# One-hot gathers on TensorE: 12 of 26 columns with the penalty in three spare rows, in place of 10 or 11 columns with a ninth matmul

## The chip, the cores and the metric

The kernel runs on one NeuronCore of a Trainium2 chip. The metric is device time in microseconds (us) of one execution. The kernel before took 16193.71 us, the median of three runs (16133.8 to 16216.83).

## The reference

A graph of 12500 nodes with 16 features and 412500 edges, sorted by destination. Three edge-conditioned convolutions (NNConv) and one maximum aggregation, with residuals:

```
def _nnconv(x, src, dst, edge_attr, ew, eb, rw, rb):
    W = (edge_attr @ ew + eb).reshape(edge_attr.shape[0], x.shape[1], rw.shape[1])
    msg = jnp.einsum('ei,eio->eo', x[src], W)
    return segment_sum(msg, dst, num_segments=x.shape[0]) + x @ rw + rb

h = relu(layernorm(x))
for i in range(2): h = relu(batchnorm(nnconv_i(h)))
h = relu(nnconv_2(h));  x = x + h @ pred_w + pred_b
h = relu(layernorm(x))
x = x + segment_max(h[src] * weight, dst) @ W.T + b
```

`ew` has 8 edge features, so an edge's message is a sum over 8 features and a bias of a row of 9 x 16 values that depends on the source node alone.

## The kernel before, in words

The padded edges are 128 streams (one a partition) of 3224 edges. A chunk is 26 columns, 26 edges of each stream; there are 124 chunks, handled two at a time (slots 0 and 1). Every column needs for each of its 128 edges the row of the edge's source node. It gets it in one of two ways.

- The first columns (16 of 26 in the convolutions, 15 in the maximum) are gathered by GpSimd: one indirect DMA a column (line 541), from a table of 144 values a node in HBM (`conv_table`) or of 16 values a node (`max_table`). VectorE releases a slot's next gathers by writing `idx` (line 968), after it has read the gathered columns.
- The last columns (10 in the convolutions, `TP_CONV`; 11 in the maximum, `TP_MAX`) are picked on TensorE from `h`, which lies in SBUF as 128 lanes by 98 blocks of 128 nodes, split in two fp32r parts (`parts`). The 98 blocks are four zones of 25. For each column, `pe_step` multiplies a one-hot matrix over (lane, zone) with the 25 blocks of that zone, for four zones and two parts: eight matmuls of 400 columns (line 712). The sum holds, for each edge, its lane's row in 25 blocks. A ninth matmul in bf16 (line 714) puts a very large negative number on the 24 wrong blocks, and VectorE takes the maximum over the blocks (`pick`, line 845). In PSUM four banks take turns, so step j waits for the pick of step j - 4.

In the convolutions a picked column has only `h`. `pe_turn` (line 723) transposes a half of the picked columns (a lot of five), ScalarE copies the transpose to `xeT` (`act_turn`, line 783), and `pe_product` (line 733) multiplies it with the edge weights, in pieces of three and two columns, fp32 in two passes each. VectorE multiplies these with the edge features (`lot_product`).

ScalarE makes the one-hot matrices for the next chunk of the same slot: four times an `Abs` of key minus lane number (line 592, the lane number a per-partition operand) and a `Relu` of 1 minus that (line 597, constants), 1408 wide whatever `TP_CONV` is, and the `Abs` for the ninth matmul (line 608). In order, `act_body` does: the first lot's `xeT` copy, the factors and flags, the store of the run, a wait until all steps of this chunk have left `hot_key` free, the one-hots of zones 0 and 1 (`hots_begin`), the second lot's `xeT` copy, and zones 2 and 3 (`hots_end`). TensorE in the same stretch does the first four steps of the next chunk, with the second lot's transpose after two of them, and then that lot's product.

The keys are rows of HBM (`key_rows`), broadcast by one DMA for two chunks to 128 partitions (`load_keys`, line 582), issued by SyncE once `hot_key` of both slots is written.

VectorE multiplies and sums the features and scans the chunk (line 952). After the 124 chunks `nodes` gathers each node's end of segment: 98 more gathers, in groups of 7 blocks (`GB`), and `node_product` makes the next table, again in groups of 7. All of the order is written out by hand.

## Time and profile before

| | before |
|---|---|
| median of 3 runs | 16193.71 us |
| span of the profiled execution | 10810.0 us |
| TensorE busy, share | 90% |
| GpSimd busy, share | 73% |
| ScalarE, VectorE busy, share | 65%, 61% |
| mean granted TensorE clock | 0.969 |

The span runs from the first to the last instruction of the one execution that was profiled. That execution's own time outside the span is in no view: only the span of 10810.0 us is. The runs' median is 5383.7 us above the span. Busy GpSimd time is that of the gathers' issue; about 0.3 us lie between two of them and count as idle. The trace has three stretches of 124 chunks for the convolutions, about 2510 us each, one of about 2380 us for the maximum, and about 200 us between two of them.

### The profile page before, as it was taken

The numbers are of one execution on the slowest core, as the hardware profiler recorded it, in microseconds if no ns is written. First come the engines' busy times: TensorE is split into PE (matmuls) and PEld (weight loads), VectorE is DVE, ScalarE is ACT, GpSimd is POOL, SyncE is SP. The second block draws the span as 40 slices with busy tenths as digits, with TensorE's granted clock in tenths as the row PEclk, the third lists the DMA queues.
The fourth block names the chain that finished last, engine by engine and source line by source line (L and its number), as shares of the span: only waits on it lengthen the run. The fifth ranks groups of instructions, "written<-read, shape, count | busy, mean of one in ns | idle before, by whom it ended". The sixth has DMA issues, their size and how long they took to land.

```text
span 10810.0 us, 169480 instructions
## 1 busy us (share of the span) xinstructions
PE 9676.4 (90%) x50106; PEld 8184.1 (76%) x50106; DVE 6568.9 (61%) x10058; ACT 7050.4 (65%) x7269; POOL 7931.6 (73%) x8306
## 2 busy tenths in 40 slices
PE   6999999998599999999849999999984999999994
PEld 4888888887488888888738888888873888888883
DVE  6677677776477677677646777776772444444442
ACT  3776776775367766767537767767763777777772
POOL 7777777777577777777757777777776777777776
PEclk9999999999799999999979999999997999999997
DMA  4333333333233333333323333333331222222221
GB/s 118 111 105 112 111 105 111 112 105 101 75 110 107 111 108 110 111 107 110 96 78 107 111 110 107 111 110 107 111 97 35 56 56 56 56 56 56 56 56 26
DMA packets 427085, 997.76 MB, mean 92 GB/s; under 512 B 167103, under 2 KB 266760, under 8 KB 395047
## 3 DMA queue, kind: packets, MB, share of 16 engines
q0 software_dynamic: 265664, 460.92, 18.3%
q1 hardware_dynamic: 161383, 536.39, 14.6%
q8 instruction: 16, 0.26, 0.0%
q14 instruction: 22, 0.18, 0.0%
HBM read 867.11 MB, written 129.62 MB: 92 GB/s over the span
## 4 chain that ended last, share of the span: by engine, by line
POOL 52%; issue 27%; DVE 10%; DMA 8%; PE 2%; DVEq 1%; POOLq 0%; ACT 0%; SPq 0%; ACTq 0%
POOL gathered L541 51%; DVE msg L927 8%; DMA gathered<-conv_table,idx 7%; PE pY L712 1%; DVE xe L845 1%; DVE idx L968 1%; PE pY L458 1%; DVEq L234 1%; POOL gathered L1108 1%; DVE gathered L270 0%; DMA conv_w<-in_conv_w 0%; DMA gathered<-scanned,idx 0%; DVE tmp L270 0%; PE pY L733 0%; PE pT L447 0%
## 5 line engine op out<-in xcount | busy, mean ns | idle before, releaser
L712 PE MATMUL pY<-part,hot_key 128*128 128x400 f32 x40672 | 8622.4, 362 | 438.0 <-DVE xe L845 409.4
L712 PEld LDWEIGHTS pY<-part,hot_key 128*128 128x128 f32 x40672 | 7322.9, 189 | 712.9 <-DVE xe L845 544.9
L541 POOL DMA_INDIRECT gathered<-conv_table,idx x5952 | 5639.3, 947 | 2030.4 <-issue 1810.9
L845 DVE TENSOR_REDUCE xe<-pY 128x16 f32<-128x400 f32 x5084 | 2834.9, 567 | 1348.9 <-PE pY L714 1334.0
L592 ACT ACTIVATE apart<-key_pair,zone_lane 128x1408 f16<-128x1408 f16 x1984 | 2804.2, 1461 | 670.5 <-PE pY L714 661.7
L597 ACT ACTIVATE hot_key<-apart 128x1408 fp32r<-128x1408 f16 x1984 | 2611.7, 1364 | 0.0
L541 POOL DMA_INDIRECT gathered<-max_table,idx x1860 | 1813.8, 975 | 611.5 <-issue 566.6
L270 DVE TENSOR_TENSOR gathered<-gathered,pT 128x2048 f32<-128x2048 f32 x372 | 851.2, 2288 | 1508.8 <-DMA gathered<-conv_table,idx 1508.8
L714 PE MATMUL pY<-near_mask,not_near 128*128 128x400 bf16 x5084 | 1747.0, 344 | 0.0
L927 DVE TENSOR_REDUCE msg<-gathered 128x256 f32<-128x2304 f32 x744 | 1559.4, 2096 | 0.2
L714 PEld LDWEIGHTS pY<-near_mask,not_near 128*128 128x128 bf16 x5084 | 488.6, 96 | 898.0 <-issue 898.0
L813 ACT COPY run_pair<-rows 128x416 f32<-128x416 f32 x496 | 491.8, 992 | 1019.3 <-DVE rows L952 1006.3
L783 ACT COPY xeT<-pT 80x128 f32<-80x128 f32 x744 | 186.6, 251 | 1363.1 <-PE pT L723 1359.2
L733 PE MATMUL pY<-edge_w,xeT 80*128 80x432 f32 (+1 forms) x2976 | 1024.5, 466 | 1.5 <-ACT xeT L783 1.5
L733 PEld LDWEIGHTS pY<-edge_w,xeT 80*128 80x128 f32 x2976 | 556.9, 193 | 261.2 <-issue 259.1
L608 ACT ACTIVATE not_near<-key_pair,zone_lane 128x1408 bf16<-128x1408 f16 x496 | 721.7, 1455 | 0.0
L270 DVE TENSOR_TENSOR gathered<-pY,pe_attr 128x432 f32<-128x432 f32 x1488 | 716.7, 524 | 3.6 <-ACT pe_attr L796 2.0
L270 DVE TENSOR_TENSOR msg<-gathered,pT 128x240 f32<-128x240 f32 x124 | 75.5, 609 | 715.0 <-DMA gathered<-max_table,idx 715.0
L952 DVE TENSOR_TENSOR_SCAN rows<-flags,msg 128x416 f32<-128x416 bf16 x496 | 503.5, 1015 | 0.1
L541 POOL DMA_INDIRECT gathered<-scanned,idx x392 | 373.6, 953 | 173.7 <-issue 116.7
L562 ACT COPY idx<-ends_i 128x7 int32 x56 | 10.6, 196 | 434.9 <-DVE agg L270 325.0
L447 PE MATMUL pT<-ident,hs 128*113 128x128 f32 x70 | 26.2, 388 | 287.2 <-ACT hs L422 284.1
(132 smaller groups left out, 1728.4 us busy)
## 6 DMA issues: line engine op xcount, KB each, us to landing
key_pair<-key_rows SPq DMA_DIRECT2D x248, 1408.0 KB, 6.3
scanned<-run_pair SPq DMA_DIRECT2D x248, 416.0 KB, 2.5
gathered<-conv_table,idx POOLq DMA_INDIRECT x5952
attr_pair<-in_attr SPq DMA_DIRECT2D x186, 208.0 KB
gathered<-max_table,idx POOLq DMA_INDIRECT x1860
conv_table<-gathered SPq DMA_DIRECT2D x24, 504.0 KB, 3.6
conv_table<-rows SPq DMA_DIRECT2D x18, 504.0 KB, 3.2
gathered<-scanned,idx POOLq DMA_INDIRECT x392, 2.3
```

What stands on the lines that cost most here:

```text
L270: return e.tensor_tensor(out, a, b, op)
L541: e.indirect_dma_start(out=G[s][:, t, 0:width], out_offset=None, in_=table[:, :], in_offset=bass.IndirectOffsetOnAxis(ap=idx[s][:, t:t + 1 ...
L592: e.activation(apart[k][:, :], keys[s][:, :], ACT.Abs, bias=zone_lane[:, z:z + 1]).then_inc(s_abs.sem, 1)
L597: e.activation(hot_key[s][:, z, :], apart[k][:, :], ACT.Relu, bias=1.0, scale=-1.0).then_inc(s_abs.sem, 1)
L608: e.activation(not_near[s][:, :], nears[s][:, :], ACT.Abs, bias=zone_lane[:, ZONES:ZONES + 1], scale=FAR).then_inc(s_hotk[s].sem, 1)
L712: e.matmul(pG[bank], hot_key[s][:, z, at:at + P], part[:, z * NEAR:(z + 1) * NEAR, :], start=(z == 0 and k == 0), stop=False)
L714: e.matmul(pG[bank], not_near[s][:, at:at + P], near_mask[:, :, :], start=False, stop=True).then_inc(s_gath.sem, 1)
L733: ins = e.matmul(pE[:, q, 0:m * ROW], xeT[:, :], edge_w[:, k * ROW:(k + m) * ROW], start=True, stop=True)
L813: e.copy(run[s][:, :, :], scan[s][:, :, :].rearrange("p d t -> p t d")).then_inc(s_run[s].sem, 1)
L845: e.tensor_reduce(xe[s][:, j * D:(j + 1) * D], pG[j % BANKS].rearrange("p (r d) -> p d r", d=D), AX.X, ALU.max).then_inc(s_pick.sem, 1)
L927: return mark(e.tensor_reduce(rows_of(a, b), g[:, a:b, :].rearrange("p t (d f) -> p t d f", f=FB), AX.X, ALU.add))
L952: e.tensor_tensor_scan(flat(scan[s]), flat(flags[s]), flat(msg), 0.0, ALU.add if is_max else ALU.mult, ALU.max if is_max else ALU.add).the ...
```

## The change

Nodes lie on 125 lanes of 100 blocks (node = lane x 100 + block), so three of TensorE's 128 contraction rows are spare. Three rows of `parts[0]` hold, for the three base-4 digits of the block within its zone, a minus one where the digit is the zone's number; the one-hot matrix's rows 125 to 127 hold a very large number where the edge's digit differs. So the eight matmuls add the penalty, and the ninth matmul, its bf16 matrix and its `Abs` go. The `Relu` takes its scale and bias from a per-partition table (`hot_line`), since three rows need others. All stages have 12 picked columns (14 gathered), in two lots of six (pieces of three and three), `hot_key` is 1536 wide, and groups have 5 blocks in place of 7 (20 groups in place of 14). The keys of a pair of chunks come by five DMAs: 112 partitions, 13 partitions, and three of one partition. The node tables' rows lie lane by lane. The zeroing of padded nodes in the last block goes, the look-up of segment ends runs one group ahead and uses other buffers, and the keys are made by rounding and digits.

```
-NB = -(-N // P)
+ZONES = 4
+NEAR = 25
+NB = ZONES * NEAR
+LANES = N // NB
+DIGITS = P - LANES
-GB = 7
+GB = 5
-TP_CONV, TP_MAX = 10, 11
+TP_CONV, TP_MAX = 12, 12
-TH = TP_CONV // 2
+TH = -(-TP_CONV // 2)
-PIECES = [(k, min(3, TH - k)) for k in range(0, TH, 3)]
+PIECES = [[(k, min(3, b - a - k)) for k in range(0, b - a, 3)] for a, b in LOTS]
...
         def load_keys(e, keyed, n):
-            e.dma_start(key_pair[:, :, :, :].rearrange("p s k e -> p (s k e)"),
-                        key_pairs[bass.ds(n, 1), :].to_broadcast([P, SLOTS * 2 * PE_EDGES])
-                        ).then_inc(keyed.sem, 16)
+            flat = key_pair[:, :, :].rearrange("p s e -> p (s e)")
+            wide = P - 16
+            for a, b in ((0, wide), (wide, LANES)):
+                e.dma_start(flat[a:b, :], key_pairs[bass.ds(n, 1), :].to_broadcast([b - a, SLOTS * PE_EDGES])
+                            ).then_inc(keyed.sem, 16)
+            for k in range(DIGITS):
+                e.dma_start(flat[LANES + k:LANES + k + 1, :], key_pairs[bass.ds(n + (1 + k) * (CHUNKS // SLOTS), 1), :]
+                            ).then_inc(keyed.sem, 16)
...
-                e.activation(hot_key[s][:, z, :], apart[k][:, :], ACT.Relu, bias=1.0, scale=-1.0
-                             ).then_inc(s_abs.sem, 1)
+                ins = e.activation(hot_key[s][:, z, cols], apart[k][:, cols], ACT.Relu, bias=hot_line[:, 1:2],
+                                   scale=hot_line[:, 0:1])
+                ins.then_inc(s_abs.sem, 1)
...
             hot_zones(e, i * SLOTS + s, s, (2, 3), b_abs, tp)
-            e.activation(not_near[s][:, :], nears[s][:, :], ACT.Abs,
-                         bias=zone_lane[:, ZONES:ZONES + 1], scale=FAR).then_inc(s_hotk[s].sem, 1)
+            gate(e, "act", s_abs, (i * SLOTS + s) * (2 * ZONES) + (b_abs + 2 * ZONES))
+            e.sem_inc(s_hotk[s].sem, 1)
...
                 for z in range(ZONES):
                     for k, part in enumerate(parts):
-                        e.matmul(pG[bank], hot_key[s][:, z, at:at + P],
-                                 part[:, z * NEAR:(z + 1) * NEAR, :], start=(z == 0 and k == 0), stop=False)
-                e.matmul(pG[bank], not_near[s][:, at:at + P], near_mask[:, :, :],
-                         start=False, stop=True).then_inc(s_gath.sem, 1)
+                        ins = e.matmul(pG[bank], hot_key[s][:, z, at:at + P], part[:, z * NEAR:(z + 1) * NEAR, :],
+                                       start=(z == 0 and k == 0), stop=(z == ZONES - 1 and k == 1))
+                ins.then_inc(s_gath.sem, 1)
...
             def pe_body(e, c1, c2):
-                for j in range(HEAD, HEAD + 4):
+                for j in range(HEAD, HEAD + 5):
                     pe_step(e, c1, j)
                 pe_turn(e, c1, 0)
-                pe_step(e, c1, HEAD + 4)
+                pe_step(e, c1, HEAD + 5)
                 pe_product(e, c1, 0)
-                for j in range(HEAD + 5, tp):
+                for j in range(HEAD + 6, tp):
                     pe_step(e, c1, j)
```

On TensorE, in the convolutions' loop, these rows stand from the first of the next chunk's four leading steps to the second lot's product. Before (`L712` is a step's eight matmuls, `L714` the ninth, `L723` the transpose, `L733` the product):

```order
L712 MATMUL pY<-part,hot_key 128x400 x8
L714 MATMUL pY<-near_mask,not_near 128x400
L234 REGISTER_ALU
L712 MATMUL pY<-part,hot_key 128x400 x8
L714 MATMUL pY<-near_mask,not_near 128x400
L234 REGISTER_ALU
L723 MATMUL pT<-ident,xe 80x128
...
L712 MATMUL pY<-part,hot_key 128x400 x8
L714 MATMUL pY<-near_mask,not_near 128x400
L234 REGISTER_ALU
L733 MATMUL pY<-edge_w,xeT 128x432
L733 MATMUL pY<-edge_w,xeT 128x288
```

And now, on TensorE in the same place:

```order
L727 MATMUL pY<-part,hot_key 128x400 x8
L237 REGISTER_ALU
L727 MATMUL pY<-part,hot_key 128x400 x8
L237 REGISTER_ALU
L737 MATMUL pT<-ident,xe 96x128
L237 REGISTER_ALU
L727 MATMUL pY<-part,hot_key 128x400 x8
L237 REGISTER_ALU
L727 MATMUL pY<-part,hot_key 128x400 x8
L237 REGISTER_ALU
L748 MATMUL pY<-edge_w,xeT 128x432 x2
```

Each step has lost its ninth matmul, and both pieces of the product are 432 wide.

On ScalarE in the same loop, the one-hots of a slot from `hots_begin` on, now:

```order
L606 ACTIVATE apart0<-key_pair,zone_lane 128x1536
L237 REGISTER_ALU
L606 ACTIVATE apart1<-key_pair,zone_lane 128x1536
L237 REGISTER_ALU
L611 ACTIVATE hot_key0<-apart0,hot_line 128x1536
L237 REGISTER_ALU
L611 ACTIVATE hot_key0<-apart1,hot_line 128x1536
L799 COPY xeT<-pT0 96x128
```

Before, the same eight rows stood there 1408 wide, and `hot_line` was no operand of the second pair; the `xeT` copy stands behind the same four activations as before.

## Rows read from the trace of the kernel before

**Rows 1.** The page: busy time by engine, and the chain that ended last

```profile
PE 9676.4 (90%) x50106; PEld 8184.1 (76%) x50106; DVE 6568.9 (61%) x10058; ACT 7050.4 (65%) x7269; POOL 7931.6 (73%) x8306
POOL 52%; issue 27%; DVE 10%; DMA 8%; PE 2%; DVEq 1%; POOLq 0%; ACT 0%; SPq 0%; ACTq 0%
```

**Rows 2.** Stretches: length, then busy PE, PEld, DVE, ACT, POOL; clock, DMA, GB/s

```profile
154.68:2669.34 2514.66, 2408.84 (x12371) 2020.49 (x12370) 1766.19 (x2470) 1755.32 (x1845) 1878.85 (x1983) 1.00 0.38 109
2697.00:2806.00 109.00, 0.00 (x0) 0.00 (x0) 8.24 (x26) 15.18 (x22) 82.24 (x88) 0.50 0.10 14
8278.78:10658.28 2379.50, 2271.78 (x12242) 2002.21 (x12240) 980.75 (x1975) 1659.25 (x1468) 1812.88 (x1860) 1.00 0.21 54
```

**Rows 3.** Waits, 540 to 2340 us (us in total, times, longest)

```profile
POOL gathered L541 <- issue: 433.1, 1342, 2.2
DVE gathered L270 <- DMA gathered<-conv_table,idx: 359.9, 89, 6.1
PEld pY L712 <- DVE xe L845: 100.8, 102, 1.9
```

**Rows 4.** Timeline of TensorE, 410 to 418 us (start, us, what)

```profile
410.05 0.34 PE L714 MATMUL pY<-near_mask,not_near 128*128 128x400 bf16 x1
...
413.43 0.10 PEld L714 LDWEIGHTS pY<-near_mask,not_near 128*128 128x128 bf16 x1 [0.17 <-issue]
...
415.17 0.10 PEld L714 LDWEIGHTS pY<-near_mask,not_near 128*128 128x128 bf16 x1 [0.18 <-issue]
...
416.82 0.37 PEld L733 LDWEIGHTS pY<-edge_w,xeT 80*128 80x128 f32 x2
417.00 1.38 PE L733 MATMUL pY<-edge_w,xeT 80*128 80x432 f32 x4
417.37 0.19 PEld L733 LDWEIGHTS pY<-edge_w,xeT 80*128 80x128 f32 x1 [0.17 <-issue]
417.73 0.19 PEld L733 LDWEIGHTS pY<-edge_w,xeT 80*128 80x128 f32 x1 [0.17 <-issue]
...
418.00 1.83 PE L712 MATMUL pY<-part,hot_key 128*128 128x400 f32 x8
```

**Rows 5.** Timeline of ScalarE, 410 to 417 us

```profile
410.83 2.83 ACT L592 ACTIVATE apart<-key_pair,zone_lane 128x1408 f16<-128x1408 f16 x2 [0.41 <-PE pY L714]
...
413.56 2.63 ACT L597 ACTIVATE hot_key<-apart 128x1408 fp32r<-128x1408 f16 x2
...
416.10 0.24 ACT L783 COPY xeT<-pT 80x128 f32<-80x128 f32 x1
```

**Rows 6.** Groups of instructions, 540 to 2340 us (busy, mean ns; idle before)

```profile
L592 ACT ACTIVATE apart<-key_pair,zone_lane 128x1408 f16<-128x1408 f16 x353 | 499.4, 1462 | 34.4 <-PE pY L714 34.0 <-issue 0.4
L845 DVE TENSOR_REDUCE xe<-pY 128x16 f32<-128x400 f32 x887 | 493.9, 566 | 150.8 <-PE pY L714 150.8
L597 ACT ACTIVATE hot_key<-apart 128x1408 fp32r<-128x1408 f16 x354 | 466.2, 1365 | 0.0
...
L805 ACT COPY flags<-same 128x416 bf16 x89 | 47.8, 537 | 0.0
```

**Rows 7.** Timeline, 2663 to 2700 us: TensorE waiting for an `xeT` copy

```profile
2665.86 0.26 ACT L783 COPY xeT<-pT 80x128 f32<-80x128 f32 x1 [1.66 <-PE pT L723]
2666.17 0.30 PEld L733 LDWEIGHTS pY<-edge_w,xeT 80*128 80x128 f32 x2 [0.70 <-ACT xeT L783]
```

**Rows 8.** Waits in the maximum, 8370 to 10440 us

```profile
PEld pY L712 <- DVE xe L845: 116.6, 108, 1.2
```

**Rows 9.** The keys' DMA: one issue in the timeline, and the page

```profile
403.02 0.33 SPq L582 DMA_DIRECT2D key_pair<-key_rows  x1
...
key_pair<-key_rows SPq DMA_DIRECT2D x248, 1408.0 KB, 6.3
```

**Rows 10.** Timeline: two groups' first evacuation in the table product

```profile
2838.79 0.61 DVE L493 COPY gathered<-pY 128x432 f32<-128x432 f32 x1 [0.35 <-PE pY L458]
...
2840.79 0.61 DVE L493 COPY gathered<-pY 128x432 f32<-128x432 f32 x1 [0.35 <-PE pY L458]
```

More of the change, by code:

```diff
@@ L39 @@
 W0, W1, W2 = 104, 64, 62
+KEY_LOADS = 2 + DIGITS
 LOOK = 2 * GB
@@ L139, in build @@
         parts = [sb(f"part{k}", [P, ZONES * NEAR, D], F32R) for k in range(2)]
-        zone_lane = sb("zone_lane", [P, ZONES + 1])
-        near_mask = sb("near_mask", [P, NEAR, D], BF16)
-        key_pair = sb("key_pair", [P, SLOTS, 2, PE_EDGES], F16)
-        keys, nears = ([key_pair[:, s, k, :] for s in range(SLOTS)] for k in range(2))
+        zone_lane = sb("zone_lane", [P, ZONES])
+        hot_line = sb("hot_line", [P, 2])
+        key_pair = sb("key_pair", [P, SLOTS, PE_EDGES], F16)
+        keys = [key_pair[:, s, :] for s in range(SLOTS)]
         apart = slots(sb, "apart", [P, PE_EDGES], F16)
         hot_key = slots(sb, "hot_key", [P, ZONES, PE_EDGES], F32R)
-        not_near = slots(sb, "not_near", [P, PE_EDGES], BF16)
         xe = slots(sb, "xe", [P, TP_KEYS * D])
@@ L289, in vector_start, with vector_parts, whole_parts @@
             e.wait_ge(s_init.sem, INIT_ALL - 1)
+        def vector_parts(e):
+            e.wait_ge(s_x.sem, NODE_ALL)
+            step(e, e.memset(parts[1][:, :, :].bitcast(F32), 0.0))
+            step(e, e.tensor_copy(parts[0][:, :, :], root[:, :, :]))
+        def whole_parts(e, out, of, by, middle):
+            step(e, e.tensor_scalar(out, of, by, middle, ALU.mult, ALU.add))
+            step(e, e.tensor_scalar(out, out, ROUND, None, ALU.add))
+            step(e, e.tensor_scalar(out, out, ROUND, None, ALU.subtract))
         def vector_same(e):
@@ L339, in masks_and_keys @@
             on("vector")(vector_masks)
-            v = bump(s_v)
+            v = s_v.n
+            bump(s_v, 1 + DIGITS)
             def sync_keys(e):
-                e.wait_ge(s_v.sem, v)
-                for k, half in enumerate(apart):
-                    e.dma_start(key_rows[:, k, :], half[0:CHUNKS, :]).then_inc(s_keys.sem, 16)
-                e.wait_ge(s_keys.sem, 32)
+                for k, (n, half) in enumerate(((0, apart[0]), (3, keys[1]), (1, apart[1]), (2, keys[0]))):
+                    e.wait_ge(s_v.sem, v + k + 1)
+                    e.dma_start(key_rows[n, :, :], half[0:CHUNKS, :]).then_inc(s_keys.sem, 16)
+                e.wait_ge(s_keys.sem, 16 * (1 + DIGITS))
             on("sync")(sync_keys)
@@ L634, in act @@
                 for s in range(SLOTS):
-                    hots_begin(e, keyed, 0, s, b_abs)
-                    hots_end(e, 0, s, b_abs)
+                    hots_begin(e, keyed, 0, s, b_abs, tp)
+                    hots_end(e, 0, s, b_abs, tp)
             on("scalar")(act)
@@ L731, in pe_product @@
                 gate(e, "pe", s_multiplied, number(c) * 2 + (half + b_mul))
-                for q, (k, m) in enumerate(PIECES):
-                    ins = e.matmul(pE[:, q, 0:m * ROW], xeT[:, :], edge_w[:, k * ROW:(k + m) * ROW],
+                deep = (LOTS[half][1] - LOTS[half][0]) * D
+                for q, (k, m) in enumerate(PIECES[half]):
+                    ins = e.matmul(pE[:, q, 0:m * ROW], xeT[0:deep, :], edge_w[0:deep, k * ROW:(k + m) * ROW],
                                    start=True, stop=True)
@@ L782, in act_turn @@
                 gate(e, "act", s_prod, number(c) * 2 + (half + b_prod))
-                e.copy(xeT[:, :], pT[0][0:TH * D, 0:P]).then_inc(s_xeT.sem, 1)
+                deep = (LOTS[half][1] - LOTS[half][0]) * D
+                e.copy(xeT[0:deep, :], pT[0][0:deep, 0:P]).then_inc(s_xeT.sem, 1)
             def act_factors(e, c):
@@ L823, in act_body @@
                     gate(e, "act", s_gath, number(c1) * tp + (tp + b_gath))
-                    hots_begin(e, keyed, *c3, b_abs)
+                    hots_begin(e, keyed, *c3, b_abs, tp)
                 act_turn(e, c1, 1)
                 if c3 is not None:
-                    hots_end(e, *c3, b_abs)
+                    hots_end(e, *c3, b_abs, tp)
             def act(e):
@@ L857, in lot_product @@
                 g4 = G[s][:, :, :].rearrange("p t (d f) -> p t d f", f=FB)
-                for q, (k, m) in enumerate(PIECES):
+                for q, (k, m) in enumerate(PIECES[half]):
                     at = LOTS[half][0] + k
@@ L1419 @@
     order = np.arange(P)
+    real = order < LANES
+    near = np.arange(NEAR)
+    digit_rows = np.zeros((P, ZONES, NEAR, D), np.float32)
+    for k, digit in enumerate((near % ZONES, near // ZONES % ZONES, near // ZONES ** 2)):
+        digit_rows[LANES + k] = -(digit == np.arange(ZONES)[:, None])[:, :, None].astype(np.float32)
+    digit_rows = digit_rows.reshape(P, NB, D)
     pieces = dst.reshape(-1)[::W2].reshape(W0, W1)
@@ L1452 @@
     got = _run(nc, [arrays], core_ids=[0]).results[0]["out"]
-    return np.asarray(got).transpose(1, 0, 2).reshape(NPAD, D)[:N]
+    return np.asarray(got).reshape(NPAD, D)[:N]
```

129 lines of the change are left out of this document (61 added, 68 removed).

## The prediction, made before the changed kernel ran

> **What bounds the kernel now.** I read the page first: TensorE is busy for 90% of the span and GpSimd for 73%, yet the chain that ended last is 52% GpSimd, and 27% of it is "issue" [rows 1]. GpSimd's queue is read by start-to-start time, not by busy time. In the first convolution 1983 gathers start in 2514.66 us, 1.268 us each, so the 16 of a chunk take 20.29 us; in the maximum it is 2379.5 / 1860 = 1.279 us, and 19.19 us for 15 [rows 2]. Gathers wait for hardly anything but their own issue, while VectorE waits 360 us in 1800 for gathered data [rows 3]. GpSimd sets the period in both kinds of stage.
>
> TensorE is close behind. A step of nine matmuls takes 416.82 - 415.17 = 1.65 us, 0.183 us a matmul; the step with the transpose before it takes 415.17 - 413.43 = 1.74, so a transpose costs 0.1. The product's first pass of 432 columns takes 417.37 - 417.00 = 0.37 us and the second 0.36; a pass of 288 columns is in proportion 0.24; so a lot of five takes 0.73 + 0.48 = 1.21 us [rows 4]. In a convolution chunk TensorE needs 10 x 1.65 + 2 x 0.1 + 2 x 1.21 = 19.1 us of the 20.29. The rest it waits: 100.8 us over 89 chunks, 1.1 us each, for picks that VectorE could not do while it waited for gathers [rows 3]. 19.1 + 1.1 gives 20.2, which closes.
>
> ScalarE comes third, and it matters where it answers TensorE. The ninth matmul that ends a chunk starts at 410.05. ScalarE then does two `Abs` and two `Relu` and only then the `xeT` copy of the second lot, from 416.10 to 416.34, 6.29 us after 410.05 [rows 4, 5]. TensorE gets to the product at 416.82, 6.77 us after it: four steps and a transpose. The copy is early by 0.48 us and nobody waits.
>
> **GpSimd after.** 14 gathers a chunk. In the convolutions 14 x 1.268 = 17.8 us, below what TensorE needs even now, so GpSimd stops setting the period there. What is late next is TensorE.
>
> **TensorE after, convolutions.** 12 steps of eight matmuls: 96 x 0.183 = 17.57 us, against 90 x 0.183 = 16.47. No row shows an fp32r step without the bf16 matmul. If the ninth costs exactly its slot, a step is 1.46 us. If the change of type costs nothing extra and the eight are as now, that is also the bound from above; from below, 400 columns at the 2.4 GHz that PEclk 1.00 stands for are 0.167 us, 1.33 a step. I take 1.46, since the slots of the eight lie at that distance in the rows. Products: two lots of four passes of 432, 4 x 0.365 = 1.46 each, 2.92 against 2.42. Transposes 0.2. Sum 20.69 us a chunk, 0.4 more than the period of today.
>
> **ScalarE after, and a wait that does not exist today.** TensorE's way from the chunk's last matmul to the second product gets shorter by four ninth matmuls: 6.77 - 4 x 0.183 = 6.04 us. ScalarE's gets longer. Its cost per column: (1365 - 537) ns over 1408 - 416 columns = 0.83 ns, so 128 more columns are 0.107 us, four times, 0.43 us [rows 6]. The `Relu` gets its scale and bias from a table. The `Abs`, with one such operand, takes 1462 ns where the `Relu` with constants takes 1365 [rows 6]; 0.097 us an operand. For a scale no row shows it: its bounds are 0 and the 0.097 of a bias, and I take the latter; two operands in two `Relu` are 0.39 us. So the copy ends 6.29 + 0.43 + 0.39 = 7.11 us after the last matmul, and TensorE starts 0.05 us later, as after the copy at 2665.86 to 2666.12 [rows 7]: 7.16. TensorE waits 7.16 - 6.04 = 1.12 us in every chunk. With scale operands free, 0.93; with both free, 0.73.
>
> The Trainium skill (ScalarE: Activation LUTs, section "What ACT_TABLE_LOAD costs") says that each per-partition pointer operand of an ACTIVATE, scale or bias, adds about 93 ns to it. By that the four operands are 0.37 us in place of 0.39, and the wait 1.10; for the bias the rows agree with 97 ns, for the scale no run here shows it.
>
> The period is 20.69 + 1.12 = 21.81 us. Against 20.29: +1.52 us x 372 chunks = +565 us.
>
> **What lies beside this.** ScalarE loses the `Abs` of the ninth matmul; it is not on that way, since `hots_end` comes after the copy, and one more wait for its own last `Relu` ends there well before the next chunk's steps. VectorE has two more picks of 0.57 us and bigger lots, some 17 us of 21.8; picks no longer stand behind a late gather, and each finds its step's bank free in time when I lay out the rows' durations. The 1.1 us that TensorE waits for picks today are therefore not added again. If that cover is gone, up to 1.1 us a chunk come back.
>
> **Maximum.** No lots, no `xeT`. GpSimd 14 x 1.279 = 17.9 us; TensorE 96 x 0.183 = 17.57 where it is 99 x 0.183 = 18.1 and 1.1 of waits for picks today [rows 8], which come of GpSimd's lateness. GpSimd stays the bound by 0.3: 17.95, against 19.19, -1.24 x 124 = -154 us. Bounds: 17.57 (-201) and 17.57 + 1.08 (-67).
>
> **Between the stages.** 100 end gathers in place of 98 at 109 / 88 = 1.24 us [rows 2], four times: +10. Table product: 14 groups at 2.00 us (2838.79 to 2840.79) [rows 10] become 20. A group's fp32 columns go from 1120 to 800, with one transpose each, about 1.5 us: 30 against 28, three times with the start of two pipelines, +8. Residual products, 12 more short groups in all: +5. The start: two more look-up gathers and wider key arithmetic, some +5. I take +28, between 0 and +60.
>
> **Sum.** 10810 + 565 - 154 + 28 = 11249 us of span, +439. The span and the runs are far apart: 16193.71 - 10810.0 = 5383.7 us lie around it, of which no view shows anything. I keep them as they are: 16194 + 439 = 16633, forecast 16630.
>
> **Rivals.**
>
> *No wait for `xeT`* (price 0 in place of 1.12). For it: ScalarE's order leaves 0.48 us today. Against: the two ways differ by 1.6 us in the rows' own durations, so the estimate of both would have to be off. Then +0.4 x 372 = +149, -154, +28: +23, 16217, no change. 11%.
>
> *fp32r matmuls alone run at the column rate and ScalarE's chain is short.* This is the one on the faster side. 96 x 0.167 + 3.12 = 19.1 us; it decides from a step of 1.40 us down, and only if the copy is no later than TensorE. 372 x (19.1 - 20.29) = -443, -154, +28: 15625. Against: eight matmuls in a row stand 0.18 apart today whatever follows them. With the short step alone the wait grows as the step shrinks (7.16 - 5.5), and the period is still 20.8. 5%.
>
> *The keys come late.* Today the load is issued at 403.02 and takes 6.3 us [rows 9], and `hots_begin` starts at 410.83 [rows 5], 1.5 us after it has landed. Now four more issues of 0.33 stand in SyncE's queue, and the transfers of one partition are no broadcasts; the bytes are about half. ScalarE's window becomes about 8 us. If the last lands 10.8 us after the first issue, each pair of chunks is late by 2.8 us: +1.4 x 372 = +521 on the forecast, 17150. For it: five transfers, all of which must land. Against: half the bytes. 7%. [...]
>
> *What lies around the span is the same work at a lower pace.* If the timed runs are 1.498 times the span whatever they do, 11249 x 1.498 = 16851. For it: 5384 us is much for anything else. Against: nothing in the trace. 10%.
>
> That the kernel doesn't do what it says is excluded by the orders: the ninth matmul is gone and 14 gathers stand in the loop.
>
> **How the numbers follow.** Forecast 67%, no wait 11%, fast matmuls 5%, late keys 7%, other pace 10%. A change of 0.5%, 81 us, is what a measurement of this kernel tells from none. The forecast's own range, with its bounds (wait 0.73 to 1.3, maximum -201 to -67, gaps 0 to 60), is 16430 to 16790. To hold 8 in 10 it must take in the other pace and lean a little to the small wait: 16330 to 16870. Slower: 67 + 7 + 10, less a little for a wait below 0.3: 83%. Same 12%, faster 5%.
>
> **What would show it.** In the convolutions: a wait of TensorE's product for `xeT` of about 1.1 us in each chunk, at its second lot only; hardly a wait for picks; a period of 21.8 us; GpSimd waiting for `idx`, about 4 us a chunk; `Relu` near 1.67 us and `Abs` near 1.57. A step of TensorE of 1.46 us. In the maximum a period of 17.95 us with GpSimd at the end of the chain. The forecast is wrong if `xeT` is waited for in no chunk, or if ScalarE's first `Abs` waits for the keys.

## The result, and the profile after: faster, where slower was forecast

| | before | after |
|---|---|---|
| median beside each other | 16178.69 us (4 runs) | 15640.44 us (4 runs, 15618.56 to 15670.77) |
| ratio | 1 | 0.965, 95% interval 0.961 to 0.969 |
| span of the profiled execution | 10810.0 us | 15669.0 us |
| mean granted TensorE clock | 0.969 | 0.864 |

The forecast was 16630 us, slower. The kernel became 3.5% faster. The first thing to see is the third line: the span after is the whole of a timed run (15640 us), where the span before was 5384 us below one. Every execution on record whose span is known has it within 3 us of its time. So nothing lies "around" a span in this kernel. The profiled execution of before was a quicker one than the runs that were timed.

The experiments were run in five sets (e1 to e4, e5 to e8, e9 to e12, e13 to e16, e17 and e18), each on one chip with the kernel before beside it. The kernel before took 16061, 10815, 16085, 10805 and 10811 us in them, and all kernels of a set went with it: the same program meets two paces. I call them the quick pace and the held pace ("hold" for what makes it slower). The third set was held and the fourth, a quarter of an hour later on a chip that the record gives the same number, was quick. If that number names one chip, the pace isn't fixed to it. The times that the prediction was asked about were held; the trace that it was built on [rows 1 to 10] was quick.

The page of after, first the busy line and the clock in 40 slices:

```profile
PE 11464.9 (73%) x52012; PEld 10275.0 (66%) x52012; DVE 7133.1 (46%) x11008; ACT 7149.4 (46%) x6857; POOL 7149.0 (46%) x7448
...
PEclk9888888888688888888878888888888788888887
...
PE 49%; another core or an unknown queue 22%; issue 20%; DVE 4%; ACT 2%; ACTq 1%; POOL 0%; DVEq 0%; DMA 0%; SPq 0%; POOLq 0%
```

In [rows 1] GpSimd made up 52% of the chain; now it is 0%, and 22% is a releaser that the trace can't name. The waits of after (engine, line, what it waited for, us in total, times, longest):

```profile
ACT apart L606 <- remote: 2923.8, 274, 40.2
DVE gathered L273 <- remote: 2792.3, 283, 20.5
...
ACT xeT L799 <- remote: 2211.7, 269, 48.4
DVE xe L861 <- remote: 1886.5, 403, 15.6
```

All four are waits for results of TensorE. A window of TensorE and VectorE shows what "remote" is (start, length, engine, line, operation, count, idle before and its releaser):

```profile
2004.47 4.87 PE L727 MATMUL pY<-part,hot_key 128*128 128x400 f32 x24
2009.45 0.56 DVE L861 TENSOR_REDUCE xe<-pY 128x16 f32<-128x400 f32 x1
2010.07 1.72 PE L727 MATMUL pY<-part,hot_key 128*128 128x400 f32 x8 [0.73 <-DVE xe L861]
2014.77 0.57 DVE L861 TENSOR_REDUCE xe<-pY 128x16 f32<-128x400 f32 x1 [4.76 <-remote]
2016.25 1.54 DVE L861 TENSOR_REDUCE xe<-pY 128x16 f32<-128x400 f32 x3 [0.91 <-remote]
2016.89 0.45 PE L737 MATMUL pT<-ident,xe 128*96 128x128 f32 x1 [5.10 <-DVE xe L861]
2016.99 3.35 PE L727 MATMUL pY<-part,hot_key 128*128 128x400 f32 x9
```

Three steps stand in the first row (steps 10 and 11 of a chunk and step 0 of the next), 24 matmuls, over at 2009.3 by the records. The pick at 2009.45 is that of step 9. VectorE is free from 2010.0 and gets the first of the three results only at 2014.77. The matmuls' records, whose ends are modelled, keep their pace, and the results come over 5 us after them. Then three picks stand back to back in 1.54 us, where a step's matmuls take about 1.5 us each. So those steps had been multiplied before: what comes late is the finished result or its signal, and the trace can't tell these two apart.

How often that happens can be counted in the trace, by holding each pick for which VectorE stood idle against the recorded end of its step's last matmul. In the quick traces of before and of e17 none of them starts over 0.1 us after that end. In the trace of after 889 of 5952 picks start over 1 us after it, the median of these 5.1 us, and in e1, the kernel before at the held pace, 1327 of 5084, the median 8.1 us.

TensorE, which now waits for the picks, has no matmul from 2011.8 to 2016.9, and the clock is low when it goes on. The granted clock of the same stretch (length, busy PE, clock, DMA share, GB/s):

```profile
2000.00:2010.00 10.00, 9.34 (x48) 1.00 0.33 79
2010.00:2017.00 7.00, 1.84 (x10) 0.83 0.20 43
2017.00:2022.00 5.00, 5.00 (x17) 0.55 0.00 0
2022.00:2032.00 10.00, 9.18 (x48) 1.00 0.31 81
```

At 1.00, the level of 2.4 GHz, a slot is 0.18 us; 17 matmuls in 5 us at 0.55, near the level of 1.2 GHz, are 0.29 us each. In the quick trace of before the clock stays at 1.00 throughout a stage [rows 2].

### The profile page after: what moved, and what is told of

The parts are those of the page before. It is cut to its first block, busy times and chain, and to the rows that moved or that the text cites. A ratio compares the mean times of both kernels' runs of the same rounds, so it can differ in the third digit from the quotient of the medians.

```text
span 15669.0 us, 179363 instructions
## 1 busy us (share of the span) xinstructions
PE 11464.9 (73%) x52012; PEld 10275.0 (66%) x52012; DVE 7133.1 (46%) x11008; ACT 7149.4 (46%) x6857; POOL 7149.0 (46%) x7448
## 4 chain that ended last, share of the span: by engine, by line
PE 49%; another core or an unknown queue 22%; issue 20%; DVE 4%; ACT 2%; ACTq 1%; POOL 0%; DVEq 0%; DMA 0%; SPq 0%; POOLq 0%
PE pY L727 41%; PE pY L748 6%; DVE xe L861 1%; ACT hot_key L611 1%; PE pY L466 1%; DVE gathered L273 1%; DVE msg L943 1%; PE pT L737 0%; POOL gathered L549 0%; DVE rows L968 0%; ACT apart L606 0%; ACT run_pair L829 0%; ACT xeT L799 0%; ACTq L237 0%
## 5 line engine op out<-in xcount | busy, mean ns | idle before, releaser
L727 PE MATMUL pY<-part,hot_key 128*128 128x400 f32 x47616 | 10210.6, 375 | 1943.8 <-DVE xe L861 1446.1
L727 PEld LDWEIGHTS pY<-part,hot_key 128*128 128x128 f32 x47616 | 9444.7, 206 | 2529.2 <-DVE xe L861 1588.4
L549 POOL DMA_INDIRECT gathered<-conv_table,idx x5208 | 4981.2, 956 | 6597.6 <-DVE idx L984 4859.7
L861 DVE TENSOR_REDUCE xe<-pY 128x16 f32<-128x400 f32 x5952 | 3276.8, 568 | 4625.9 <-PE pY L727 2573.4
L606 ACT ACTIVATE apart<-key_pair,zone_lane 128x1536 f16<-128x1536 f16 x1984 | 3015.4, 1567 | 4558.4 <-remote 2923.8
L611 ACT ACTIVATE hot_key<-apart,hot_line 128x1536 fp32r<-128x1536 f16 x1984 | 3192.4, 1657 | 0.0
L748 PE MATMUL pY<-edge_w,xeT 96*128 96x432 f32 x2976 | 1471.5, 623 | 1332.5 <-issue 998.9
L748 PEld LDWEIGHTS pY<-edge_w,xeT 96*128 96x128 f32 x2976 | 588.4, 213 | 1809.5 <-issue 1804.3
L943 DVE TENSOR_REDUCE msg<-gathered 128x224 f32<-128x2016 f32 x744 | 1558.5, 2095 | 0.2
L273 DVE TENSOR_TENSOR gathered<-gathered,pT 128x1792 f32<-128x1792 f32 x372 | 749.4, 2015 | 1.8
```

The costliest lines, as they stand in the source:

```text
L273: return e.tensor_tensor(out, a, b, op)
L549: e.indirect_dma_start(out=G[s][:, t, 0:width], out_offset=None, in_=table[:, :], in_offset=bass.IndirectOffsetOnAxis(ap=idx[s][:, t:t + 1 ...
L606: e.activation(apart[k][:, cols], keys[s][:, cols], ACT.Abs, bias=zone_lane[:, z:z + 1]).then_inc(s_abs.sem, 1)
L611: ins = e.activation(hot_key[s][:, z, cols], apart[k][:, cols], ACT.Relu, bias=hot_line[:, 1:2], scale=hot_line[:, 0:1])
L727: ins = e.matmul(pG[bank], hot_key[s][:, z, at:at + P], part[:, z * NEAR:(z + 1) * NEAR, :], start=(z == 0 and k == 0), stop=(z == ZONES - ...
L748: ins = e.matmul(pE[:, q, 0:m * ROW], xeT[0:deep, :], edge_w[0:deep, k * ROW:(k + m) * ROW], start=True, stop=True)
```

## Experiments

In the order of what they settle. "Before beside it" is the kernel before, timed on the same chip in the same set.

### The same kernels again: is the pace the kernel's?

e1 is the kernel before, e9 and e17 the changed one, with no edit.

> The kernel before, unchanged, for a profile of an execution of the usual time. Theory A (in usual executions TensorE finishes its matmuls late again and again, whatever their records say, and that sets the time): span near 16170 us, granted clock well below 0.969 (about 0.86), semaphores of a step's last matmul that come over 1 us after its recorded end in a third or more of the steps. Theory B (what lies around the span makes up the 5384 us): span near 10810 again, clock 0.97, none late.

> The changed kernel unchanged. Two theories of why it came out at 15640 us against 16179. (A) The forecast's schedule holds wherever TensorE finishes its matmuls in time, and the chips differ: where the kernel before takes about 10815 us beside it, this one takes 11250 to 11290, ratio 1.042, with TensorE's second product waiting some 1.1 us a chunk for xeT; where the kernel before takes about 16060, this one takes about 15640, ratio 0.97, and the product waits for late steps. (B) The changed kernel is faster by itself, for example by the form of its matmuls: then the ratio is below 1 beside a kernel before of 10815 us as well.

> The changed kernel unchanged. Beside a kernel before of about 10810 us: 11270, as its version with zero parts, ratio 1.042, if the schedule of the forecast is what counts there; below 10810 if the change is faster by itself. Beside about 16070 us: 15640 again.

| | this | before beside it | ratio (95%) |
|---|---|---|---|
| e1, before | 16012.59 | 16061.35 | 1.0005 (0.997 to 1.004) |
| e9, after | 15625.86 | 16085.1 | 0.971 (0.965 to 0.977) |
| e17, after | 11273.77 | 10811.33 | 1.0425 (1.0408 to 1.0443) |

The changed kernel is 3% faster at the held pace and 4.2% slower at the quick one: of each expectation the branch that ties the outcome to the pace came out, though not by the chip, as e9's text has it. e1 gives what the first trace did not: the kernel before as it was timed, as its Theory A said (late results in a quarter of the steps, where it named a third or more). Its span is 15899.5 us, and its page reads

```profile
PE 10941.9 (69%) x50106; PEld 9130.1 (57%) x50106; DVE 6710.6 (42%) x10058; ACT 7054.6 (44%) x7269; POOL 8031.6 (51%) x8306
...
PEclk8888888888788888888878888888886888888887
```

against 90% PE and 73% POOL in [rows 1]. Its first convolution and its maximum, and below them those of after in its own trace (busy PE, PEld, DVE, ACT, POOL, then the clock):

```profile
198.00:4022.00 3824.00, 2734.28 (x12392) 2262.07 (x12393) 1802.28 (x2478) 1762.34 (x1850) 1917.59 (x1984) 0.85 0.25 72
12157.00:15741.00 3584.00, 2583.62 (x12273) 2250.77 (x12274) 1031.01 (x1982) 1661.01 (x1469) 1795.52 (x1860) 0.85 0.14 36
```

```profile
242.00:4032.00 3790.00, 2896.88 (x13107) 2574.07 (x13106) 1915.77 (x2718) 1765.69 (x1721) 1661.54 (x1736) 0.89 0.23 57
12290.00:15505.00 3215.00, 2482.79 (x11901) 2381.43 (x11899) 1078.32 (x2102) 1692.18 (x1346) 1680.76 (x1736) 0.87 0.13 28
```

By 124 chunks: a convolution chunk takes 30.8 us before and 30.6 after, a chunk of the maximum 28.9 and 25.9. GpSimd's busy time is as in [rows 2]; it just waits. Without the edges of the windows, as the mean of 123 periods from the first chunk's scan to the last's, in the traces of the held pace (us a chunk; the last column is the rest of the span, in us):

| | convolution 1, 2, 3 | maximum | rest |
|---|---|---|---|
| e1, before | 30.63, 30.71, 29.94 | 28.68 | 1025 |
| e2, before, no ninth | 27.26, 28.16, 28.37 | 26.19 | 1020 |
| e3, after, 10 columns | 27.63, 27.80, 28.11 | 25.57 | 1133 |
| after | 30.44, 30.48, 30.59 | 25.71 | 1133 |
| e4, after, with a ninth | 31.24, 31.28, 31.23 | 28.12 | 1138 |

The gain lies in the maximum: 2.97 us in 124 chunks are 368 us. The three convolutions together take 29 us more after than before in these two traces, and the rest of the span 108 us more. That makes the 230 us between the two spans. The timed medians lie further apart (538 us beside each other, 459 in e9's set), and e1's profiled execution was the shortest of its ten. Between the traces of e10, which is before in a set of its own and ran as long as before, and e9 the maximum again gives some 350 us, the convolutions some 200, and the rest costs some 110. So the share of the convolutions is within the scatter of single executions, and that of the maximum is not. A window of e1 shows a long hold:

```profile
2003.41 1.76 PE L712 MATMUL pY<-part,hot_key 128*128 128x400 f32 x8
...
2009.52 1.76 PE L712 MATMUL pY<-part,hot_key 128*128 128x400 f32 x8
...
2014.76 0.94 POOL L541 DMA_INDIRECT gathered<-conv_table,idx  x1 [0.30 <-issue]
2015.39 0.58 DVE L845 TENSOR_REDUCE xe<-pY 128x16 f32<-128x400 f32 x1 [9.28 <-remote]
2018.27 0.57 DVE L845 TENSOR_REDUCE xe<-pY 128x16 f32<-128x400 f32 x1 [2.31 <-remote]
```

The step recorded at 2003.41 is picked at 2015.39, with VectorE idle for 9.28 us. GpSimd meanwhile issues a gather every 1.25 us, as at the quick pace. Only TensorE is held.

### What TensorE multiplies: e5, e6, e10

Both parts of `h` are made zero (e6 the same on the changed kernel, where the three rows of the penalty stay). The edit of e5 and e10:

```
-                step(e, e.tensor_copy(parts[0][:, 0:NB, :], h[:, :, :]))
-                step(e, tt(e, tmp[:, :, :], h[:, :, :], parts[0][:, 0:NB, :].bitcast(F32), ALU.subtract))
+                step(e, e.tensor_scalar(tmp[:, :, :], h[:, :, :], 0.0, None, ALU.mult))
+                step(e, e.tensor_copy(parts[0][:, 0:NB, :], tmp[:, :, :]))
```

> The kernel before with zeros in both parts of h, so that nearly all of TensorE's products are zero; instructions and shapes as before. Theory H (TensorE is held back by what it computes, not by the schedule): near 10810 us, clock 0.97, as the one profiled execution of before. Theory N (what slows the usual executions has nothing to do with the operands): 16000.

> The changed kernel with zeros in both parts (the penalty's rows stay). Theory H: TensorE is free, and the prediction's own sum of the schedule holds: 11250 us, slower than e5 by 4%, with TensorE waiting about 1.1 us a chunk for the xeT copy. Theory N: 15640.

> The kernel before with both fp32r parts of h zero, so that TensorE multiplies by zeros and the output is not the reference's. It was 10812 us beside a kernel before of 10815. Beside a kernel before of about 16060 us: if the late completions of TensorE come of the energy or the value of its operands, it falls to some 10800 to 13000; if they do not depend on what is multiplied, it stays within 0.5% of 16060. Beside 10815 us it says nothing new, 10812.

The set of e5 and e6 met the quick pace: 10811.82 (ratio 0.9997) and 11270.16 us (1.042). Both numbers are those that Theory H named, and only the kernel before beside them, unedited and at 10814.77, shows that the zeros had no part in it. e10 met the held pace: 16066.93 beside 16085.1, ratio 0.999 (0.995 to 1.003). With zeros for `h` TensorE is held just as much. The one-hot matrices were not zero in any run.

### How much TensorE does: e2, e3, e4, e13

e2 is the kernel before without its ninth matmul (the 24 wrong blocks stay in the maximum). e3 is the changed kernel with `TP_CONV` 10. e4 adds a ninth bf16 matmul of zeros to it. e13 does the first part of `h` alone. Of each edit the line that matters:

```
e2  -                e.matmul(pG[bank], not_near[s][:, at:at + P], near_mask[:, :, :],
    -                         start=False, stop=True).then_inc(s_gath.sem, 1)
e3  +TP_CONV, TP_MAX = 10, 12
e4  +                e.matmul(pG[bank], ident[:, :].bitcast(BF16)[:, 0:P], nothing[:, :, :],
    +                         start=False, stop=True).then_inc(s_gath.sem, 1)
e13 +                    for k, part in enumerate(parts[0:1]):
```

> Leaves out the bf16 matmul that masks the wrong blocks (its ScalarE work stays), 9 to 8 matmuls a step. Theory A: TensorE's work falls by about 10%, time 14600 to 15200. Theory B, GpSimd sets the period as in the profile of before: 16180, no change. Theory C, the bf16 matmul between fp32r ones costs more than its slot: below 14600.

> The changed kernel with 10 of 26 columns on TensorE in the convolutions (lots of five), 12 in the maximum. Theory A: TensorE's work in the convolutions falls by a sixth, time 13400 to 14200. Theory B, the move of two columns from GpSimd to TensorE is what gained: 16000 or more.

> The changed kernel with a ninth bf16 matmul of 400 columns in each step again, on a zero tile, so that it adds nothing; no ScalarE work for it. Theory A: 12% more TensorE work in the steps, time 16700 to 17400. Theory B (the ninth is free beside what sets the time): 15640.

> The changed kernel with the four matmuls of the first part of h alone in a step, so that the second part of each picked value is left out. Scheduled TensorE time per chunk is 6.6 us less for 48 matmuls in a convolution: 8.8 + 3.1 = 11.9 us, 8.8 in the maximum; GpSimd's 14 gathers need 17.5 to 17.9. Beside a kernel before of about 16070 us: if TensorE is late in proportion to its matmuls (1.48 to 1.6 times the schedule, 17.6 to 19 us), GpSimd sets the period and it takes 9700 to 10300; if it loses a fixed 10 us a chunk, 22 us a chunk in the convolutions and 19 in the maximum, it takes 11400 to 11800. Beside 10815 us: 9700 to 9900 either way.

| | this | before beside it | ratio (95%) |
|---|---|---|---|
| e2, before, no ninth | 14492.03 | 16061.35 | 0.903 (0.899 to 0.907) |
| e3, after, 10 columns | 14667.26 | 16061.35 | 0.914 (0.910 to 0.918) |
| e4, after, with a ninth | 16316.76 | 16061.35 | 1.018 (1.014 to 1.022) |
| e13, after, half the matmuls | 10156.41 | 10804.9 | 0.940 (0.938 to 0.941) |

At the held pace the time goes up and down with TensorE's work. That splits the change in three: without its ninth matmul alone the kernel before has a ratio of 0.903 (e2); the rest of the change with ten columns in the convolutions brings that to 0.914 (e3); and the two more columns there bring it to 0.971 (e9). Seen from the other side, the rest of the change with a ninth matmul is slower, 1.018 (e4). By stage, in the table above: the ninth is worth some 2.5 us a chunk in both kinds, the two columns cost some 2.6 in a convolution, and in the maximum one column more with one gather less costs nothing. The sizes were not those expected. e2 is below the range of Theory A and in that of Theory C, e3 lies between its two theories (14667 against 13400 to 14200), and so does e4 (16317 against 16700 to 17400). The price of a matmul isn't constant. Of 5084 ninths taken from before each is worth 1569 / 5084 = 0.31 us, more than its slot of 0.183 [rows 4]; of 5952 added to the changed kernel each costs (1.018 - 0.971) x 16061 / 5952 = 0.13 us; and the 5952 matmuls of two columns in three stages, products included, (0.971 - 0.914) x 16061 / 5952 = 0.15 us. Of these three the last two lie within the runs' intervals of each other and the first doesn't. No run shows why it is dearer.

e13 met the quick pace and says nothing on the hold. But it shows that a low clock is not the hold: with half the matmuls, and TensorE waiting up to 5.6 us for `xeT`, the clock falls with no "remote" wait, and none of its picks is late. Its time was 10156 where 9700 to 9900 was expected: a convolution chunk takes 18.7 us where GpSimd's 14 gathers need 17.5, and why was not looked into. Its clock:

```profile
PEclk9888888887688888888858888888886777777776
```

### The turn of the banks: e7, e11

With 10 columns and banks `j % 4`, two steps a chunk wait for a pick two back; with 12 columns none does. (With the 11 columns of the maximum before, three steps wait for a pick three back.) e7 and e11 take 10 columns in the convolutions and let the banks turn across chunks:

```
+TP_CONV, TP_MAX = 10, 12
+                return (c[1] * tp + j) % BANKS
```

> The changed kernel with 10 columns in the convolutions as in e3, but the four PSUM banks taken in turn across chunks, so that a step always waits for the pick four steps back (in e3 the first two steps of a chunk wait for picks two steps back). Theory R (with 12 columns the banks come round evenly, which is why its matmuls take 0.27 us a piece where those of 10 and 11 columns take 0.29 to 0.30): 13700 to 14000. Theory S (the spacing has another cause): 14667.

> The changed kernel with 10 picked columns in the convolutions and the four PSUM banks taken in turn across chunks, so that every step waits for the pick four steps back. It was 10740 us beside a kernel before of 10815. Beside a kernel before of about 16060: if the better ratio of 12-column stages there comes of the even turn of the banks (with 10 columns, two steps a chunk wait for a pick two back), it takes 13700 to 14200, well below the 14667 of the version with 10 columns and uneven banks; if the amount of matmuls alone sets the time, 14600 to 14700.

e7's two theories were for the held pace. It took, at the quick pace, 10740.39 us beside 10814.77, ratio 0.993 (0.992 to 0.995); at the held one 14709.08 beside 16085.1, ratio 0.917 (0.909 to 0.924), the same as e3 without that turn. So the turn of the banks is not what makes a convolution chunk of 12 columns lose less. For the 11 columns of the maximum, where the gain lies, no run tested it. This version beats both kernels at both paces, the kernel before by only 0.7% at the quick one.

### ScalarE's way to the copy: e8, e12

```
-                ins = e.activation(hot_key[s][:, z, cols], apart[k][:, cols], ACT.Relu, bias=hot_line[:, 1:2],
-                                   scale=hot_line[:, 0:1])
+                ins = e.activation(hot_key[s][:, z, cols], apart[k][:, cols], ACT.Relu, bias=1.0, scale=-1.0)
```

Both leave the penalty out of the products.

> The changed kernel with the Relu's scale and bias as constants, so that the three rows hold no penalty (picks of wrong blocks are let through). The prediction's theory (the copy behind ScalarE's four activations is what TensorE waits for): 0.39 us a chunk less, -145 us, 15500. Theory A (TensorE's own hold sets the time): 15640, no change beyond 0.3%.

> The changed kernel with the scale and bias of the Relu as constants, which leaves the penalty out of the products. It was 11135 us, 135 less than with the two per-partition operands, beside a kernel before of 10815. Beside a kernel before of about 16060: if TensorE's late completions set the period there and ScalarE's chain has room, it is within 0.5% of the changed kernel in this set (15640); if the xeT wait is paid there too, it is 130 to 150 us below it.

Quick: 11135.13 us, 135 below e6. Held: 15617.03, 9 below e9 and inside its scatter. That is e12's first branch: the copy of `xeT` costs time only where TensorE gets to it on time.

### The gathers, and the type: e15, e16, e18, e14

e15 and e18 (the changed kernel) and e16 (before) issue 2 gathers a chunk; e14 has one-hots and parts in bf16. Parts of the edits:

```
+ISSUED = 2
+                        for t in range(ISSUED):
...
-        hot_key = slots(sb, "hot_key", [P, ZONES, PE_EDGES], F32R)
+        hot_key = slots(sb, "hot_key", [P, ZONES, PE_EDGES], BF16)
```

> The changed kernel with two gathers issued of the 14 of a chunk, so that the other columns' values are stale. TensorE's work is unchanged. Beside a kernel before of about 16070 us: if only TensorE's own matmuls count, 15640 within 1.5%; if each gather holds it up by about 0.7 to 1 us, 12 x 0.7 x 496 = 4200 us less, about 11500 (TensorE's schedule of 20.7 us a chunk is the floor). Beside 10815 us: 11100 to 11270, since gathers are not the bound there.

> The changed kernel with two gathers issued of the 14 of a chunk, the other columns stale. Beside a kernel before of about 16070 us: 15640 within 1.5% if only TensorE's own matmuls count; about 11500 if each gather holds it up by 0.7 us or more. Beside 10810 us: 11213 again.

> The kernel before with two gathers issued of the 15 or 16 of a chunk, the other columns stale. TensorE then hardly waits for picks that stand behind late gathers. Beside a kernel before of about 16070 us: if only its matmuls count, 16070 within 1.5%; if it is the starts after such waits that cost, the ratio to the schedule falls from 1.61 to the 1.48 of the changed kernel, 28.3 us a chunk, about 14900 to 15100; if the gathers themselves hold it up, below 12000. Beside 10815 us: TensorE's 19.1 us a chunk and a little, 10200 to 10400.

> The changed kernel with the one-hot matrices and both parts of h in bf16 in place of fp32r, which rounds the values; number, width and order of the matmuls are the same. Beside a kernel before of about 16070 us: if the amount of matmuls makes TensorE late, 15640 within 2%; if the fp32r form does, it falls towards what the quick chip showed, 11300 to 12500. Beside 10815 us: 11000 to 11300.

All four met the quick pace: 11213.36, 11212.47, 10199.57 and 10964.61 us. Whether gathers or the fp32r form have part in the hold, which they were made for, stays open. As forecasts of the quick pace the gathers' ranges held (e16 at its lower edge), and e14 fell 35 us below its own. What they do say is on the schedule. Stretches of e16, then of e18, from the first chunk's scan to the last's, 123 periods each:

```profile
181.22:2522.35 2341.13, 2334.38 (x12230) 1993.57 (x12228) 1800.99 (x2453) 1724.44 (x1827) 228.39 (x242) 1.00 0.18 61
7831.90:10049.96 2218.06, 2215.88 (x12112) 1979.27 (x12110) 1041.30 (x1961) 1633.25 (x1459) 228.18 (x242) 1.00 0.17 52
```

```profile
193.43:2863.81 2670.38, 2555.98 (x12972) 2331.74 (x12970) 1907.51 (x2698) 1749.63 (x1706) 228.25 (x242) 1.00 0.13 39
8916.75:11058.24 2141.49, 2137.68 (x11741) 2137.23 (x11739) 1104.52 (x2081) 1678.03 (x1339) 228.12 (x242) 1.00 0.12 36
```

Without gathers a chunk of before is TensorE alone: 2341.13 / 123 = 19.03 us, where the prediction's rows gave 19.1. The maximum is 18.03, where they gave 18.1. In the changed kernel the convolution does not move, 21.71 us with two gathers or fourteen, so GpSimd had left its path as forecast; the maximum goes from 17.92 to 17.41, so GpSimd was its bound, as forecast too. In bf16 the period of a convolution chunk is 20.87 us in place of 21.71, with the same count and width of matmuls. A slot is read best from the weight loads (PEld), one before each matmul, since the ends of the matmuls' rows are modelled. 39 matmuls in a row in e14, then a row of e18's maximum:

```profile
419.23 6.53 PEld L730 LDWEIGHTS pY<-narrow,hot_key 128*128 128x128 bf16 x39 [0.27 <-issue]
```

```profile
9999.83 40.25 PEld L728 LDWEIGHTS pY<-part,hot_key 128*128 128x128 f32 x221
```

From 419.23 to the next load at 425.82 a bf16 slot is 0.169 us; an fp32r slot is 40.25 / 221 = 0.182. A part of what the shorter slots give goes to a longer wait for `xeT`, 482.1 us in 369 waits, 1.31 each.

## Why the prediction was wrong, by its own steps

**The step that failed** is the last of the sum: "The span and the runs are far apart: 5383.7 us lie around it, of which no view shows anything. I keep them as they are." They were not around the span. They lay inside the runs, about 10.6 us in every convolution chunk (30.84 against 20.28) and 9.7 in the maximum, as TensorE's lateness, and they changed with the change. The rival "same work at a lower pace" (10%) was nearer in kind and further off in number (16851): it multiplied the quick schedule, GpSimd's share of it included, by 1.498 and so came out slower. At the held pace GpSimd's 16 gathers (20.3 us) are far inside a period of 30.8 us. Taking gathers off GpSimd is no gain that shows there. The ninth matmuls come off the engine that sets the time, 2.5 us a chunk (e1 and e2). In the convolutions the two columns more take that back (e3 and after), and in the maximum it stays as the gain.

**The sum itself held where its trace was valid.** e17 is the changed kernel at the pace of that trace, and its span is 11273.0 us against the 11249 of the sum. That is closer than its terms: the convolutions came out 37 us below the sum and the rest of the span 56 above it. Its waits from 540 to 2340 us, the stretch of [rows 3]:

```profile
POOL gathered L549 <- DVE idx L984: 352.1, 82, 4.7
...
PE pY L748 <- ACT xeT L799: 73.5, 82, 0.9
```

and TensorE, its weight loads and ScalarE around one second lot, to be read against [rows 4, 5]:

```profile
420.64 3.17 PE L727 MATMUL pY<-part,hot_key 128*128 128x400 f32 x16
424.67 1.71 PE L748 MATMUL pY<-edge_w,xeT 96*128 96x432 f32 x4 [0.85 <-ACT xeT L799]
425.88 7.79 PE L727 MATMUL pY<-part,hot_key 128*128 128x400 f32 x40
```

```profile
425.13 0.19 PEld L748 LDWEIGHTS pY<-edge_w,xeT 96*128 96x128 f32 x1 [0.17 <-issue]
425.49 0.19 PEld L748 LDWEIGHTS pY<-edge_w,xeT 96*128 96x128 f32 x1 [0.17 <-issue]
425.86 0.19 PEld L727 LDWEIGHTS pY<-part,hot_key 128*128 128x128 f32 x1 [0.17 <-issue]
426.22 7.10 PEld L727 LDWEIGHTS pY<-part,hot_key 128*128 128x128 f32 x39 [0.17 <-issue]
433.32 0.12 PEld L737 LDWEIGHTS pT<-ident,xe 128*96 128x96 f32 x1
```

```profile
418.23 3.04 ACT L606 ACTIVATE apart<-key_pair,zone_lane 128x1536 f16<-128x1536 f16 x2 [4.02 <-PE pY L727]
421.18 3.22 ACT L611 ACTIVATE hot_key<-apart,hot_line 128x1536 fp32r<-128x1536 f16 x2
424.30 0.24 ACT L799 COPY xeT<-pT 96x128 f32<-96x128 f32 x1
```

- *A new wait of 1.12 us a chunk for `xeT`, at the second lot only*: right in place; 73.5 / 82 = 0.90 us. Sized 0.2 too high, since TensorE's way there is longer than I took it.
- *A step of 1.46 us*: right. From 426.22 to 433.32 are 39 slots in 7.10 us, 0.182 each, 1.46 a step. The row of 40 matmuls at 425.88 begins too early to be divided by 40: it overlaps the product's last pass.
- *Two products of 1.46 us*: right. The loads at 425.13, 425.49, 425.86 and 426.22 stand 0.36 to 0.37 apart, a pass each, so four passes are 1.46.
- *A transpose of 0.1 us*: too short. From 433.32 to the load of the next matmul at 433.50 it takes a slot of its own, 0.18, so two are 0.16 us a chunk more, about the difference between a schedule of 21.71 - 0.90 = 20.81 us and the 20.69 of the sum.
- *Period 21.81 us*: 21.71, mean of 123 periods. *GpSimd waits some 4 us a chunk for `idx`*: 352.1 / 82 = 4.3.
- *`Relu` 1.67 us, `Abs` 1.57, both operands at 0.097*: 1657 ns and 1567 ns. e8 has the same `Relu` with constants; the last line below is e8's, the first e17's:

```profile
L611 ACT ACTIVATE hot_key<-apart,hot_line 128x1536 fp32r<-128x1536 f16 x1984 | 3192.3, 1657 | 0.0
```

```profile
L611 ACT ACTIVATE hot_key<-apart 128x1536 fp32r<-128x1536 f16 x1984 | 2825.5, 1473 | 0.0
```

  184 ns for two operands, 92 each, so a scale costs what a bias does. The Trainium skill (ScalarE: Activation LUTs, section "What ACT_TABLE_LOAD costs") says about 93 ns for each pointer operand; the trace agrees. Forecast gain of e8 145 us, measured 135.
- *Maximum 17.95 us, GpSimd's bound*: 17.92, and e18 shows what was behind it: TensorE at 17.41, where 17.57 was summed.
- *+28 us between the stages*: measured 11273 - 3 x 124 x 21.71 - 124 x 17.92 = 975, against 10810 - 3 x 124 x 20.27 - 124 x 19.18 = 891 before; +84. The edge of its range of 0 to 60 was passed.
- *Late keys* (7%): they do come late, but only in the maximum, the first line below. The prediction named this as a sign that it was wrong. It cost nothing: e18 has more such waits in its maximum, the second line, and its period of 17.41 us is TensorE's 96 slots of 0.181. In the convolutions no `Abs` waits for keys.

```profile
ACT apart L606 <- DMA key_pair<-key_rows: 199.5, 50, 5.1
```

```profile
ACT apart L607 <- DMA key_pair<-key_rows: 215.2, 60, 4.1
```

- *No wait for `xeT`* and *matmuls at column rate* (11% and 5%) are refuted at the quick pace, by the 0.90 us and the 0.182 us.

So mechanism, places and signs were right for an execution that is not the one timed. The warning stood in the table of times: 5384 us, a third of the time, had no row. It was the largest unknown of the sum, and I gave it 10%. That the timed runs had another bound was no rival at all.

**Still open.** What holds TensorE, and why it meets some sets of runs and not others: not the values of `h` (e10), not the turn of the banks in the convolutions (e11), not ScalarE's way to the copy (e12), nor, by the record's numbers, the chip. What the other cores of the chip did during the runs is not on record, so their load is a rival that nothing here tests. What the traces show is the shape of the loss. Against TensorE's own schedule at the quick pace (19.03 and 18.03 us before, 20.81 and 17.41 after) the held pace adds 11.4 us to a convolution chunk before and 9.7 after, and 10.6 and 8.3 in the maximum: roughly a fixed price a chunk, with the matmuls on top. The late picks also stand at a fixed place in the chunk: in the maximum of after 396 of 410 are those of steps 7 to 11. Why a chunk with 12 columns and 14 gathers loses less than one with 10 or 11 and 16 or 15 was not settled. Fewer gathers, fewer stops of TensorE and, in the maximum, the turn of the banks fit. The runs that would tell the first met the quick pace.

## What to carry to other kernels

Before summing anything, hold the span of the profiled execution against the timed runs. Where they differ by more than the runs' scatter, the profile is of another execution, its bound may be another engine, and no term of it may be kept "as it is". A trace of a kernel that is timed in two paces needs a forecast for each: here the change as a whole loses 4% in one and wins 3% in the other, while with 10 columns in the convolutions and the banks in turn it wins in both (0.993 and 0.917). And an edit that comes out at the number its theory named proves nothing until the unedited kernel of the same set is beside it (e5).

## What the runs showed of the hardware

- One program on one core takes 10805 to 10815 us or 16061 to 16179 us (medians of the sets), and the pace holds for all kernels of a set. The mean granted clock is 0.969 against 0.837 for the kernel before, which is 14% lower and can't make a run 48% longer: in 1327 of 5084 steps TensorE's result comes over 1 us late, the median of these 8.1 us (e1).
- The Trainium skill (TensorE: Matmul & The Clock Gate, section "Seeing it yourself") describes a peak-current limiter that takes the clock to 13/16, that one or two busy cores never trip and that all-zero operands don't trip either. In the traces of the held pace the granted clock is 1.0 or 0.5 and never 13/16, and zeros for `h` changed nothing (ratio 0.999). So the hold doesn't look like that limiter; what it is isn't shown.
- An fp32r matmul of 400 columns takes a slot of 0.182 us in long rows (e17, e18), the same as with a bf16 one after every eighth (0.183, [rows 4]); in bf16 it takes 0.169 (e14).
- A transpose between such matmuls takes 0.18 us (e17), as much as a matmul of 400 columns.
